# A mixture-of-experts and attention block on one core: attention scores computed on 64-row halves of the array

## What is computed

```
q, k = rope(x @ W_q.T), rope(x @ W_k.T)      # 16 heads of 8
scores = einsum('blhd,bshd->bhls', q, k) / sqrt(8)
weights = softmax(scores, axis=-1)
out = einsum('bhls,bshd->blhd', weights, v).reshape(B, L, 128)
return out @ W_o.T
```

## Time and profile before

| | |
|---|---|
| median of 3 runs | 422.71 us (421.59 to 426.31) |
| profiled execution, its span | 422.1 us |
| TensorE busy | 312.1 us, 74% |
| VectorE busy | 232.4 us, 55% |
| ScalarE busy | 200.6 us, 48% |
| GpSimd busy | 176.9 us, 42% |
| mean granted TensorE clock | 0.929 |
| attention | about 121 to 316 us |
| a steady turn of attention | 21.5 us |

### The profile page before, as it was taken

The page is one execution under the profiler, slowest core; times in us unless marked ns, Lnnn a source line. Parts: engine busy times, 40 slices in busy tenths (PEclk is TensorE's granted clock), DMA queues, the critical chain, the costliest instruction groups (busy, mean ns, idle before and its releaser), DMA issues.

```text
span 422.1 us, 6677 instructions
## 1 busy us (share of the span) xinstructions
PE 312.1 (74%) x2088; PEld 173.7 (41%) x2105; DVE 232.4 (55%) x573; ACT 200.6 (48%) x451; POOL 176.9 (42%) x341
## 2 busy tenths in 40 slices
PE   1769939878615697989797989888775993988760
PEld 0135615545413343545454545444441552545440
DVE  8946303233235878787878786887744640233322
ACT  1116104333404568686868777876560720344420
POOL 3915723455626525242424342430211473266550
PEclk9999978899955899999999999999997998899995
DMA  7950151000030000000000000000000015100017
GB/s 222 188 220 31 52 157 20 25 33 31 37 106 0 1 2 2 1 2 2 2 0 2 2 0 2 2 3 1 2 2 0 25 50 148 35 26 31 31 40 205
DMA packets 24269, 18.34 MB, mean 43 GB/s; under 512 B 4944, under 2 KB 22608, under 8 KB 23984
## 3 DMA queue, kind: packets, MB, share of 16 engines
q1 hardware_dynamic: 21744, 12.84, 12.0%
q0 software_dynamic: 2496, 5.13, 3.4%
HBM read 10.26 MB, written 7.71 MB: 43 GB/s over the span
## 4 chain that ended last, share of the span: by engine, by line
PE 34%; DVE 26%; POOL 13%; issue 11%; ACT 7%; DMA 6%; another core or an unknown queue 1%; SPq 1%; POOLq 0%; DVEq 0%; ACTq 0%
PE bank L846 25%; DVE negmax L739 11%; DVE xn L603 5%; POOL xs_sorted L346 5%; PE bank L1005 3%; ACT xs L495 2%; POOL y_by_token L366 2%; DMA xs<-y_by_token 2%; PE bank L966 2%; PE bank L942 2%; DVE rs L755 1%; DVE qT L732 1%; DMA xg<-xs_sorted 1%; DVE stats L613 1%; DVE rh L704 1%
## 5 line engine op out<-in xcount | busy, mean ns | idle before, releaser
L739 DVE TENSOR_REDUCE negmax<-bank 128x2 f32<-128x512 f32 x128 | 81.8, 682 | 13.8 <-PE bank L846 10.0
L535 ACT ACTIVATE probs<-bank 128x512 f32<-128x512 f32 x128 | 72.1, 606 | 26.0 <-PE bank L846 25.5
L846 PE MATMUL bank<-rgu,xgT 128*128 x92 | 53.3, 663 | 16.2 <-issue 13.7
L366 POOL DMA_INDIRECT y_by_token<-ys,xg x46 | 44.9, 977 | 45.0 <-PE bank L942 19.8
L704 DVE TENSOR_TENSOR rh<-rsg,bank 128x256 f32<-128x256 f32 x46 | 19.4, 421 | 79.6 <-ACT rsg L513 79.6
L846 PE MATMUL bank<-qT,kT 128*128 128x256 bf16 x256 | 48.9, 273 | 9.5 <-DVE qT L732 3.9
L846 PE MATMUL bank<-kT,qT 128*128 128x512 bf16 x112 | 43.3, 387 | 9.5 <-DVE negmax L739 5.7
L513 ACT ACTIVATE rsg<-bank 128x256 f32<-128x256 f32 x46 | 17.7, 384 | 61.7 <-PE bank L846 61.7
L346 POOL DMA_INDIRECT xs_sorted<-xs,slot x32 | 31.5, 984 | 34.5 <-ACT xs L495 26.6
L543 ACT COPY kT<-bank 64x1024 bf16<-64x1024 bf16 x32 | 32.2, 1006 | 19.7 <-PE bank L1005 19.5
L846 PE MATMUL bank<-probs,vx 128*32 128x256 f32 x512 | 39.0, 389 | 0.1
(11 more groups left out here) (107 smaller groups left out, 477.4 us busy)
## 6 DMA issues: line engine op xcount, KB each, us to landing
xg<-xs_sorted SPq DMA_DIRECT2D x10, 258.0 KB, 4.0
rgu<-in_rgu SPq DMA_DIRECT2D x1, 2048.0 KB, 19.5
xs<-y_by_token SPq DMA_DIRECT2D x8, 256.0 KB, 3.7
xs_sorted<-xg SPq DMA_DIRECT2D x1, 1483.5 KB, 15.6
x<-in_x SPq DMA_DIRECT2D x4, 256.0 KB, 3.5
rdn<-in_rdn SPq DMA_DIRECT2D x1, 1024.0 KB, 15.7
out_x<-x SPq DMA_DIRECT2D x4, 256.0 KB, 2.6
y_by_token<-ys,xg POOLq DMA_INDIRECT x46
```

Of the source, the lines that this page charges most:

```text
L366: g.indirect_dma_start(y_dram, bass.IndirectOffsetOnAxis(ap=xg[:, j, D:ROW].bitcast(U32), axis=0), ys[:, j, :], None, bounds_check=N + SLO ...
L535: a.activation(probs[:, h % 8, :], stbank[st_bank(u, h)][:], ACT.Exp, scale=float(DH) ** -0.5).then_inc(exp_done, 1)
L739: v_.tensor_reduce(negmax[:, w, t, h0 + 2 * pair:h0 + 2 * pair + 2], sbank[k % 2][:].rearrange("p (a s) -> p a s", a=2), AX.X, ALU.max, ne ...
L846: return t_.matmul(o_, l, r, start=start, stop=stop, **k)
```

## The change

kT loses its dimension of 2 and with it the zero halves and their two memsets. ScalarE copies a half's keys with one instruction on 128 partitions. Each product of scores now has both operands on the 64 partitions of its head. scores goes head by head: two products of 256 columns (both query tiles of one head) instead of one of 512 columns (two heads, one query tile). In a slot the two kinds alternate: scores_t tile 0, scores tile 0, scores_t tile 1, scores tile 1; score_head swaps neighbouring heads, so that scores works on the other 64 rows than scores_t in the same slot. Both waits of a slot now stand ahead of its four products, and the values of slots 6 and 7 stand behind them.

```diff
-        kT = [sb(f"kT{u}", [P, H // 2, 2, L], BF16) for u in range(2)]
+        kT = [sb(f"kT{u}", [P, H // 2, L], BF16) for u in range(2)]
...
+        def score_head(k):
+
+            return 2 * (k // 2) + 1 - k % 2
...
-                g.memset(kT[u][:].bitcast(F32), 0.0).then_inc(consts_set, 1)
...
-                    src = work[uses.index(name) % 2][:].bitcast(BF16).rearrange("p (r s) -> p r s", r=4)
-                    for k in range(2):
-                        ins = a.copy(kT[v][64 * k:64 * k + 64, 4 * half:4 * half + 4, k, :], src[64 * k:64 * k + 64])
-                    ins.then_inc(emptied[name], 1)
+                    a.copy(kT[v][:, 4 * half:4 * half + 4, :].rearrange("p r s -> p (r s)"),
+                           work[uses.index(name) % 2][:].bitcast(BF16)).then_inc(emptied[name], 1)
...
-                    pair, t = k // 2, k % 2
-                    v_.tensor_reduce(negmax[:, w, t, h0 + 2 * pair:h0 + 2 * pair + 2], sbank[k % 2][:].rearrange("p (a s) -> p a s", a=2),
+                    v_.tensor_reduce(negmax[:, w, :, h0 + score_head(k)], sbank[k % 2][:].rearrange("p (t s) -> p t s", t=2),
                                      AX.X, ALU.max, negate=True).then_inc(s_reduced, 1)
...
-                    pair, t = k // 2, k % 2
-                    mm(sbank[k % 2][:], qT[w][:, h0 + pair, t * P:(t + 1) * P],
-                       kT[w][:, h0 + pair, :, :].rearrange("p a s -> p (a s)")).then_inc(s_filled, 1)
-
-                def scores_t(h):
+
+                def scores(half, k, t):
+
+                    w, h = (u, HH + score_head(k)) if half == 0 else (v, score_head(k))
+                    rows = slice(64 * (h % 2), 64 * (h % 2) + 64)
+                    ins = mm(sbank[k % 2][:, t * L:(t + 1) * L], qT[w][rows, h // 2, t * P:(t + 1) * P], kT[w][rows, h // 2, :])
+                    if t:
+                        ins.then_inc(s_filled, 1)
+
+                def scores_t_free(h):
...
-                    for k in range(2):
-                        ins = mm(stbank[st_bank(u, h)][:, k * L:(k + 1) * L], kT[u][:, h // 2, h % 2, k * P:(k + 1) * P], qT[u][:, h // 2, :])
-                    ins.then_inc(st_filled, 1)
+
+                def scores_t(h, k):
+
+                    rows = slice(64 * (h % 2), 64 * (h % 2) + 64)
+                    ins = mm(stbank[st_bank(u, h)][:, k * L:(k + 1) * L], kT[u][rows, h // 2, k * P:(k + 1) * P], qT[u][rows, h // 2, :])
+                    if k:
+                        ins.then_inc(st_filled, 1)
...
                         if T.e:
-                            scores_t(HH * half + s_)
-                            if s_ in (6, 7):
-                                values(2 * half, int(s_ == 7))
+                            scores_t_free(HH * half + s_)
                         if (T.m if half else T.e):
-                            scores(half, s_)
+                            scores_free(half, s_)
+                        for k in range(2):
+                            if T.e:
+                                scores_t(HH * half + s_, k)
+                            if (T.m if half else T.e):
+                                scores(half, s_, k)
+                        if T.e and s_ in (6, 7):
+                            values(2 * half, int(s_ == 7))
```

More of the change, by code:

```diff
@@ L373, in _ @@
             for u in range(2):
-                g.memset(kT[u][:].bitcast(F32), 0.0).then_inc(consts_set, 1)
                 g.memset(vx[u][:], 0.0).then_inc(consts_set, 1)
                 g.memset(parts[u][:].bitcast(F32), 0.0).then_inc(consts_set, 1)
-            pool.wait_ge(consts_set, 7)
+            pool.wait_ge(consts_set, 5)
             for u in range(2):
@@ L1006, in turn_parts, with scores_free @@
                     ins.then_inc(filled[name], 1)
-                def scores(half, k):
-                    w, h0, unit = (u, 4, 2 * i + 1) if half == 0 else (v, 0, 2 * i + 2)
+                def scores_free(half, k):
+                    unit = 2 * i + 1 if half == 0 else 2 * i + 2
                     if k == 0:
```

## The result

The changed kernel takes 431.73 us (median of 4 runs, 429.84 to 433.18) where the kernel before took 424.51 in the same comparison: a ratio of 1.0157, interval 1.0111 to 1.0204. It is slower by 1.6%; the forecast was 418 us and a range of 412 to 429. The profiled execution has a span of 428.2 us.

What follows compares the result with a forecast made beforehand. VectorE was taken to bound the first half and the second until slot 5's maximum, then TensorE's program order. Gains less losses summed to 4.8 us: 422.1 to 417.3, median 0.6 above, called 418; range 412 to 429.

Steps and rivals of the forecast that it cites:

- clock 1.00 through attention: Sign of a right forecast in the new profile: TensorE's granted clock stays at full speed throughout attention.
- a rival with a chance of 0.10: Sparser TensorE work between rope and slot 5 drops the clock: +2.0 us a turn, 432 us; chance 0.10.
- (a): Start of a turn: first scores after the copies take 0.45 us instead of 0.65, gaining 0.20 in eight turns.
- (b): VectorE-bound slots of the first half: no loss, and a smaller gap around slot 3's transposes, gaining 0.06 us.
- (c): End of the first half: values of chunk 1 behind the last scores delay turning "mb", losing 0.2 us.
- (d): Tail of the second half from slot 5: 2.58 us against 3.31, gaining 0.73 in seven turns.
- (e): Second half: scores_t(8) waits for rope, ScalarE runs 0.3 us late; cost taken as 0.1 in seven turns.
- the rival on switches: Each change between 64-row and full-width work costs 0.20 us, not 0.10: 422 us; chance 0.25 shared with half overlap or cover.
- (f): ScalarE's keys in one copy: 1.0 us off each half, but covered by other waits, so worth 0.
- (g): Zeroing of kT leaves GpSimd at the start, which idles 12.48 us before its first scatter: worth 0.
- The rival of halves in turn: TensorE does not overlap the row halves, a slot takes 0.43 us: 7 us lost, 429 us; chance 0.12.
- the forecast's question: Whether two row halves run at once on TensorE; a slot's four products bounded at 0.22 to 0.43 us, taken as 0.25.

Runs made afterwards that it cites:

- e2_halves: The changed kernel with the old order of products, values and separate waits, keeping 64-row products and one key copy; ratio 1.0511 to the kernel before.
- e4_in_turn: The changed kernel with score_head(k) = k, so both kinds of a slot use the same 64 rows and cannot overlap; ratio 1.0968 to the kernel before.
- e5_tail: The kernel before with scores ahead of the values in slots 6 and 7 of the second half only; 421.23 us against 426.30, ratio 0.9879.
- e10_clock_values: e6_keep_clock with scores_t and values of slots 6 and 7 of the first half ahead of the bank wait; ran once, steady turn 21.09 us.
- e11_full_rows: e4_in_turn with every score product on all 128 rows, zero halves in the keys and two key copies; ratio 1.0198 to the kernel before.
- e1_order: The kernel before with only the new order of waits, scores and values, on 128 rows with zero halves and two key copies; ratio 1.0101.
- e6_keep_clock: The changed kernel with one unused full-width product of 256 columns added in slots 0 to 4 of each half; ratio 1.0084 to the kernel before.
- e9_clock_not_held: e6_keep_clock with scores_t in slots 0 and 1 of the second half ahead of the wait for rope; ran once, steady turn 21.72 us.

## Why the prediction was wrong

**The step that failed is the one on the clock.** The sum that gives 418 has no term for it, "clock 1.00 through attention" was forecast, and the fall stood only as a rival with a chance of 0.10. The fall came, and the four turns that it hit lost 8.2 of the 8.8 us in attention. The rival had the mechanism, its place (between rope and slot 5 of the second half) and its sign. The text put the new work of the array at 35% of that stretch, by counting a pair abreast as one product; the rows it had to judge this by were a stretch of 21% that was followed by a fall and two that held, 55% and a short one of 2 us. A value between them was read as if it belonged to the upper one. The lower one was also read too low: TensorE's weight loads show six score products in 137.88 to 143.15, the record of the first being missing, which makes 6 x 0.22 of 5.27 us, 25%. And e2_halves and e4_in_turn show that time occupied was the wrong thing to count. Their products run mostly or wholly one behind the other and occupy TensorE about as long as before, and the clock falls more often than in the change itself. The 64-row form does it without any overlap, 27.41 against 22.35 us a turn. Then its size: it was priced at +2.0 us in a turn that is hit. It hit turns 0, 1, 3 and 6, for 1.05 and 1.06 in the steady ones (1.23 against a turn of the same kernel at the full clock) and for 3.7 and 2.4 at the start and the end, where I had not looked. At the full clock a turn gains 0.18 us; over seven turns that is an estimate of 1.3 us for the change without the falls, against the 4.8 forecast.

**The turn itself was also over-priced.** At the full clock it is 21.32 us where the steps give 20.8 (21.5 less 0.73, 0.20 and 0.06, plus 0.20 and 0.1). Term by term, from one chain to the other:

| step | forecast | measured, full clock |
|---|---|---|
| (a) first scores after "ma" is copied | -0.20 | -0.19 (1.40 to 1.21, from copy to first maximum) |
| (b) maxima of the first half | -0.06 | +0.18 (6.00 to 6.18) |
| (c) last maximum to turning "mb" | +0.20 | +0.40 (1.35 to 1.75) |
| (d) slot 5 to the last maximum | -0.73 | -0.62 (3.31 to 2.69) |
| (d), (e) last maximum to the copy of "ma" | +0.1 | +0.23 (2.70 to 2.93) |
| first maximum of the second half to slot 5 | 0 | -0.18 (3.52 to 3.34) |

(a) and (d) were right in mechanism and nearly in size, and the halves do run abreast. Yet e5_tail has all of (d)'s gain without them: the likeliest term of the forecast was order, and I credited it to both. Of (c) I had half; e10_clock_values shows that putting the values back returns 0.48. Two sizes lie behind (b) and (c). Going back from full-width to 64-row work costs more than going there: 208.28 + 0.11 to 208.48 is 0.09, but the projection then takes 0.64 to the next score product instead of the 0.44 of the earlier trace rows, so 0.20, and the transposes at 210.02 take 0.37 instead of 0.22, so 0.15. I had 0.10 for each way, 0.20 for going there and back; it is 0.29 here, halfway to the 0.40 of the rival on switches. The Trainium skill, "TensorEngine Tiling (Array Packing)", Key Properties, that changing the mode drains the engine, agrees with these rows. And a slot starts 0.14 us after the maximum that frees its bank, where 0.05 was assumed; e11_full_rows has that too on 128 rows, so it is not the row halves. What sets it wasn't tried.

**(e)** was right that ScalarE would be late and become the neighbour of the bound, and the chain of waits has it as the bound. Freeing it brought nothing; VectorE's xn and GpSimd then collide, a second cover that was not in the text at all. The -0.18 in the table's last row comes with that collision's absence (xn 0.59 instead of 1.04).

**(f)** was right only by its neighbours. With one key copy of 1.0 us it costs nothing and gains nothing in the changed kernel; with two, in the same order, it holds the turn's first products (e1_order), so the edit pays for the coupling of waits that comes with it. I wrote that scores_t(0) was covered, and it is, by this edit. **(g)** held: GpSimd idled 12.57 us ahead of its first scatter.

**The rival of halves in turn** did not come true, since the halves overlap. e4_in_turn makes its condition: I had 429, it took 468. With the clock held by full rows the same order takes 1.0198 of the kernel before (e11_full_rows), 8 us more, where the rival had 7: its price was near, but it too had no term for the clock.

So the answer to the forecast's question is: the overlap is real and worth 22.35 - 21.32 = 1.0 us a turn against the same order on full rows (the key copies included; xn takes 0.6 us in both), the order costs 0.7 (22.22 against 21.50), and the clock takes back more than what is left. Even with the clock held (e6_keep_clock) the steady turns gain nothing. Turn 0 is the turn with the fewest products (178 records against 196), and its low clock begins before it: it falls at 137.8 and comes back at 154.9, where the kernel before had it low from 144.0 to 147.4, and it is low again from 161.7 to 168.6. On full rows in e4_in_turn's order turn 0 keeps the full clock (e11_full_rows, 21.53 us). Why it stays low so long on 64 rows, with added products too, is open.

## What to carry to other kernels

Before a product is made smaller on the array, look at what holds the granted clock: where the engine is only partly busy, rows of zeros can be what keeps it at full speed, and an edit that saves array time off the critical path can gain nothing there and lose by the clock. When a record of the trace is what such a judgement rests on, count the weight loads as well as the products. Split a change that mixes order and form into its parts: here the order of two instructions in one half of the turn gave 1.2%, and the rest cost more than it brought. When several waits are put in front of a group, price each cover again, since the slowest of them now holds all.

## What the runs showed of the hardware

- Products on rows 0 to 63 and 64 to 127 that write to different banks start within 0.02 us of each other and hold the array as long as one (0.10 to 0.12 us for 256 bf16 columns at the full clock).
- The granted clock fell with 64-row products (27.41 us a turn, mean clock 0.81) and stayed at 1.00 with the same products in the same order on 128 rows of which half hold zeros (22.35 us; two key copies instead of one).
- One full-width product of 256 columns in ten of sixteen slots was enough to hold it in the steady turns of e6_keep_clock (21.57 us, clock 1.00) and e10_clock_values (21.09 us), not in turn 0, and not in turn 2 of e9_clock_not_held (23.18 us, clock 0.93).
- VectorE's TENSOR_SCALAR on 128x128 fp32, two in a row, took 0.59 us alone and 0.95 to 1.04 beside a GpSimd TENSOR_TENSOR; moving it out of the way confirmed it (0.59 again).
- ScalarE's copy of bf16 keys takes 1.0 us for 1024 columns on 64 partitions and the same on 128 (two copies in 2.02 in the earlier trace rows):

```profile
L544 ACT COPY kT<-bank x16: 1012/1012/1012, 133.0 to 299.1; 128x1024 bf16<-128x1024 bf16 x16
```
